# 128-wide attention: projections that begin with half of the turned tiles, a place of their own for the first values' weights, and bias additions inside the first head

## The reference

```python
x = x + _L0_attn_a_ref(_layernorm(x, axis=-1), ...)   # 32 heads of width 16
x = x + _L0_ffn_ref(_layernorm(x, axis=-1), ...)
x = x + _L0_attn_b_ref(_layernorm(x, axis=-1), ...)
x = x + _L0_ffn_ref(_layernorm(x, axis=-1), ...)
x = x + _L1_attn_a_ref(_layernorm(x, axis=-1), ...)   # the step that changes
x = x + _L1_ffn_ref(_layernorm(x, axis=-1), ...)
x = x + _L1_attn_b_ref(_layernorm(x, axis=-1), ...)
x = x + _L1_ffn_ref(_layernorm(x, axis=-1), ...)
```

```python
q = hidden_states @ Wq + bq          # 32 heads of 128
k = hidden_states @ Wk + bk          #  8 heads of 128
v = hidden_states @ Wv + bv          #  8 heads of 128
...                                  # _rope(x): [x1 cos - x2 sin, x1 sin + x2 cos]
scores = einsum('bgrsd,bgtd->bgrst', qg, k) / sqrt(128)
probs = softmax(where(causal, scores, lowest))
ctx = einsum('bgrst,bgtd->bgrsd', probs, v)
return ctx @ Wo + bo
```

## Time and profile before

| what | us |
|---|---|
| median of three runs | 2809.57 (2801.65 to 2809.91) |
| the profiled execution | 2806.13 |
| its span, first to last instruction | 2804.4 |
| the stage of the 128-wide attention, start of its first transfer | 598.0 |
| its last scores | 1654.0 |

### The profile page before, as it was taken

The page is one execution under the profiler, slowest core; times in us unless marked ns, Lnnn a source line. Parts: engine busy times, 40 slices in busy tenths (PEclk is TensorE's granted clock), DMA queues, the critical chain, the costliest instruction groups (busy, mean ns, idle before and its releaser), DMA issues. The chain is left out here.

```text
span 2804.4 us, 41981 instructions
## 1 busy us (share of the span) xinstructions
PE 2549.3 (91%) x14502; PEld 1758.5 (63%) x14502; DVE 1904.1 (68%) x3382; ACT 1495.5 (53%) x2528; POOL 824.3 (29%) x777
## 2 busy tenths in 40 slices
PE   7899988878999999999999987899878999868995
PEld 5444444546888888888888864566554454445663
DVE  6888623445767777777777676677678886366774
ACT  5677821215555555555555541466447778315663
POOL 1200001024535344534345310355412000004552
PEclk9899998989999999999999997999988999889998
DMA  4000000010000000000000012988820000229887
GB/s 156 1 1 1 1 18 20 18 38 23 23 17 27 16 23 24 20 23 23 16 23 23 13 44 86 326 213 196 181 95 1 1 2 1 98 105 313 196 202 205
DMA packets 68190, 197.42 MB, mean 70 GB/s; under 512 B 9040, under 2 KB 9936, under 8 KB 62608
## 3 DMA queue, kind: packets, MB, share of 16 engines
q1 hardware_dynamic: 46928, 145.44, 15.3%
q0 software_dynamic: 21056, 49.30, 9.4%
HBM read 154.33 MB, written 40.37 MB: 69 GB/s over the span
## 5 line engine op out<-in xcount | busy, mean ns | idle before, releaser
L1430 ACT ACTIVATE L1a_ph<-single 128x512 fp32r<-128x512 f32 (+3 forms) x384 | 174.4, 489 | 180.0 <-PE single L1517 179.3
L1571 DVE TENSOR_TENSOR L1a_pl<-single,L1a_ph 128x512 fp32r<-128x512 f32 (+3 forms) x384 | 199.6, 549 | 52.7 <-ACT L1a_ph L1430 52.1
L1587 DVE SCALAR_TENSOR_TENSOR x<-single,L1a_rinv,x 128x512 f32<-128x512 f32 x256 | 189.5, 745 | 58.5 <-PE single L1181 58.2
L1421 ACT ACTIVATE L1a_probs<-pair,L1a_least 128x128 f32<-128x128 f32 (+7 forms) x256 | 190.1, 744 | 71.4 <-DVE L1a_least L1565 69.8
L1565 DVE TENSOR_REDUCE L1a_least<-pair 128x1 f32<-128x128 f32 (+7 forms) x256 | 190.8, 751 | 42.8 <-PE pair L1506 42.2
L1398 POOL TENSOR_TENSOR L1a_swapped<-L1a_swapped,L1a_sin 128x512 f32<-128x512 f32 x80 | 129.2, 1615 | 302.5 <-ACT L1a_swapped L1462 302.5
L793 DVE TENSOR_REDUCE L0a_least<-single 128x1 f32<-128x512 f32 (+3 forms) x304 | 186.4, 658 | 37.6 <-PE single L615 20.7
L793 DVE TENSOR_REDUCE L1b_least<-single 128x1 f32<-128x512 f32 (+3 forms) x304 | 186.2, 657 | 37.8 <-PE single L615 20.8
L496 ACT ACTIVATE L0a_probsT<-pair 128x896 f32<-128x896 f32 (+2 forms) x192 | 149.0, 811 | 59.2 <-PE pair L635 47.1
L496 ACT ACTIVATE L1b_probsT<-pair 128x896 f32<-128x896 f32 (+2 forms) x192 | 149.0, 811 | 59.2 <-PE pair L635 47.0
L1517 PE MATMUL single<-ident,L1a_probs 128*128 128x128 f32 x1152 | 168.9, 274 | 1.4 <-ACT L1a_probs L1421 1.4
(11 more groups left out here) (517 smaller groups left out, 6931.0 us busy)
## 6 DMA issues: line engine op xcount, KB each, us to landing
L1f_wd<-in_L1f_w SPq DMA_DIRECT2D x48, 512.0 KB
L1g_wd<-in_L1f_w SPq DMA_DIRECT2D x48, 512.0 KB
L1a_raw<-in_L1a_w SPq DMA_DIRECT2D x80, 256.0 KB, 2.6
L1f_store<-in_L1f_w SPq DMA_DIRECT2D x16, 1024.0 KB, 8.4
L1g_store<-in_L1f_w SPq DMA_DIRECT2D x16, 1024.0 KB, 9.2
sum<-L0a_pad_row SPq DMA_DIRECT2D x2, 2304.0 KB, 16.4
sum<-x SPq DMA_DIRECT2D x16, 256.0 KB
x<-sum SPq DMA_DIRECT2D x16, 256.0 KB, 5.0
```

The lines of the kernel that those rows point to most:

```text
L1421: act.activation(probs[:, u % 2, 0:n], g.pair[u % 2][:, 0:n], ACT.Exp, bias=least[:, u % 4:u % 4 + 1], scale=-1.0, accum_out=rsum[:, h % 2 ...
L1430: act.activation(p_tile(ph, u, i), turned_bank(u, i), ACT.Copy).then_inc(p_high, 1)
L1571: dve.tensor_tensor(p_tile(pl, u, i), turned_bank(u, i), p_tile(ph, u, i).bitcast(F32), ALU.subtract)\
L1587: dve.scalar_tensor_tensor(out=g.x[:, t, :], in0=aux_bank(("O", h, t)), scalar=rinv[:, h % 2, t:t + 1], in1=g.x[:, t, :], op0=ALU.mult, op ...
```

## The change

Four things are edited, all in the stage `L1a`:

1. TensorE's turning of a tile becomes a step `x` of its table. Six tiles are turned, then comes the first keys' projection (tokens 0 to 511, which are tiles one to four), then the last two tiles. Each projection waits for the split tiles that it reads: four for a first half, eight for a second.
2. The first values' weights get the place of the odd output weights, number 4, so that they need not wait for the keys' weights. The opening now has the first values' projection and its turning, and both halves of the first queries.
3. The first head gets a table of its own, `FIRST_HEAD`; all later heads keep `SCHEDULE`.
4. GpSimd's eight bias additions go from the opening into the first head, and VectorE's output additions of that head wait for their own tile only.

```diff
 OPENING = {
-    "PE": "K0 Q0 K1 s s Q1",
-    "ACT": "K0 Q0 K1 e Q1",
-    "DVE": "K0a K0b Q0a Q0b m K1a K1b m Q1a Q1b",
-    "POOL": "w w x x x x x x x x K0a K0b Q0a Q0b K1a K1b w Q1a Q1b w w",
+    "PE": "x x x x x x K0 x x Q0 K1 V0 v0 Q1",
+    "ACT": "K0 Q0 K1 V0 v0 Q1",
+    "DVE": "K0a K0b Q0a Q0b v0 K1a m K1b Q1a m Q1b",
+    "POOL": "w w w w K0a K0b Q0a K1a Q0b w Q1a K1b Q1b",
+}
+FIRST_HEAD = {
+    "PE": ("s V1 s t s", "v1 Q0 t s", "s t Q1 W1p t s", "s t W0", "s", "O6p t O7p O5p O1 s", "O4p O0", "t s O2 t O3"),
...
+    "POOL": ("Q0a", "x x Q0b w", "x x", "x", "", "x w x", "Q1a", "x"),
 }
...
-    rows = [(-1, OPENING[engine])] + [(h, text) for h in range(HEADS128) for text in SCHEDULE[engine][h % GH]]
+    rows = [(-1, OPENING[engine])]
+    for h in range(HEADS128):
+        rows += [(h, text) for text in (SCHEDULE[engine][h % GH] if h else FIRST_HEAD[engine])]
...
-                of = {"Q": of + 1, "K": of // GH + 1}.get(kind, of // GH)
+                of = {"Q": of + 1, "K": of // GH + 1}.get(kind, max(of, 0) // GH)
...
 def weight_slot(piece):
     kind, n = piece
+    if piece == ("V", 0):
+        return 4
...
-                for t in range(NT):
-                    if t >= 2:
-                        pe.wait_ge(x_split, t - 1)
-                    ln_turn(pe, g, ln, t)
-                pe.wait_ge(x_split, NT)
...
+                    if s[0] == "x":
+                        if s[1] >= 2:
+                            pe.wait_ge(x_split, s[1] - 1)
+                        ln_turn(pe, g, ln, s[1])
+                    elif s[0] == "s":
...
                         pe.wait_ge(w_split, SPLIT_NO[piece_of(s)])
+                        pe.wait_ge(x_split, (s[2] + 1) * BLK)
...
                         if h == 0:
-                            dve.wait_ge(biased, NT)
+                            dve.wait_ge(biased, t + 1)
```

More of the change, by code:

```diff
@@ L1492, in _ @@
                         bank_free(s)
-                    if s[0] == "s":
+                    if s[0] == "x":
[3 more added lines that the diff above has]
+                    elif s[0] == "s":
                         u = s[1]
```

## The result

The change takes the median from 2809.57 us (10 runs, 2801.65 to 2814.72) to 2794.11 us (10 runs, 2790.45 to 2800.44): a ratio of 0.995, with a 95% interval of 0.9940 to 0.9961. That is 15.5 us; the interval allows 11 to 17. The forecast was 2792, between 2785 and 2800.

The account below looks back on a forecast made before the run. TensorE's idle time and low clock in the 128-wide attention's opening were taken as the loss. 4.64 + 1.12 + 38.05 + idle (2.0 + 0.5 + 0.8) = 47.1 us against 62.87, 15.8 less: 2792 us, range 2785 to 2800.

Parts of the forecast that it names:

- The sum: From the sixth turned tile's end to the second head's row: 47.1 us against 62.87 before, 15.8 us less.
- the gap for the queries: TensorE's 5.66 us idle ahead of the first scores, for rotated queries: gone, replaced by about 2.0 us before the values' transposes.
- First projection: TensorE's first keys' projection, started right behind the sixth tile at the low clock: 4.64 us, bounds 2.84 and 5.7.
- Clock behind the gap: TensorE's work after the 2.0 us gap ahead of the values' transposes was counted at full clock, a projection at 2.84 us.
- rival of the low clock: Low clock stays longer in the opening, costing 5 us: gain 10 to 11, 2796 to 2797 us; chance 0.14.
- Small waits: TensorE's remaining waits through the first head: 0.3, 0.3 and 0.2, 0.8 us in all, bounds 0 and 4.
- The rival of the softmax: Each of the first head's eight units waits 1.43 us for its exponential, costing 11.4: gain 4, 2803 us; chance 0.10.
- Keys' bias step: ScalarE's first keys' bias step starts at 622.1 us against 625.16 before, 3 us earlier, after splitting tiles seven and eight.
- The table load: ScalarE's load before the first exponential ends at 638.5 us; between 0 and 0.45 us may follow it, 0 taken.
- Hidden, with about 1.5 us to spare: GpSimd's moved additions in the first head: second head's last low queries done at 670.5 us, wanted near 672.
- the rival of a late GpSimd: GpSimd's 17 instructions slow to 1.8 us beside VectorE, late for the second head by 6 us: gain 10, 2797; chance 0.08.
- The six tiles: TensorE's turning of the first six tiles, up to 615.74 us: the change moves nothing there.

Follow-up runs that it names:

- the run with the additions in gaps: Changed kernel with GpSimd's eight bias additions moved to where GpSimd idles in the opening; stage 1054.9 us, against 1058.1 for the changed kernel.
- The run with half of the tiles alone: Kernel before with only the first projection behind six turned tiles and the other two tiles behind it; stage 1068.8 us, against 1074.5 before.
- the run with the scaling later: Changed kernel with VectorE's scaling of the query bias behind the sixth tile's split instead of ahead of the third row; stage 1059.0 us.
- the two reordered openings: Changed kernel with values projected before the second keys (stage 1057.7 us); or with additions in idle gaps, scaling later, first keys' steps before the last tiles' split (1054.4).

## Why the prediction was right, and where it was not

**The sum.** 47.1 us stood for the stretch from the sixth tile to the second head's row; 46.5, 46.2 and 46.9 were measured. The order came out as read: projection at once, tiles behind it, four pieces of weights split by 615.3, the gap for the queries gone, a gap of 2.15 us (forecast 2.0) ahead of the transposes. The terms were less exact than the sum:

- First projection: taken as 4.64, measured 3.88 (615.56 to 619.44). The row of 0.40 at 617.81 shows the clock up 2.2 us after the start, where the earlier trace rows needed 3.93. In the other runs of this order it took 3.1 to 4.7: the same term, with a spread that a single row couldn't show.
- Clock behind the gap: taken as full, but it fell. The projection behind the transposes took 4.39 us (631.49 to 635.88) instead of 2.84, 1.55 more. This is one part of the rival of the low clock, and I had named its reason: a gap between 1.41 and 3.45. The two rows of the granted clock, before the gap's end and after it:

```profile
629.00:631.00 2.00, 0.00 (x0) 0.00 (x0) 1.12 (x2) 1.89 (x3) 0.98 (x2) 1.00 0.00 0
...
632.00:633.00 1.00, 1.00 (x4) 0.74 (x3) 0.50 (x1) 0.47 (x1) 1.00 (x2) 0.50 0.00 0
```

While TensorE idled the clock was at its upper level, and at the lower one, 1.2 GHz, when the work had started again.

- Small waits: 0.8 taken, next to none measured. TensorE is busy 20.00 of 20 us from 640 to 660. The rival of the softmax (1.43 us in each unit) is refuted by that row: in the first head no exponential but the first is waited for (0.35 us).

Too long by 0.8 and 0.8, too short by 1.55: they cancel.

**Keys' bias step.** Predicted 6.4 us behind the sixth tile's end; it came 5.1 behind it (621.04). ScalarE's rows show why:

```profile
620.07 1.09 ACT L1167 ACTIVATE L1a_xh<-single 128x512 fp32r<-128x512 f32 x2 [3.53 <-PE single L141]
621.04 0.69 ACT L1469 ACTIVATE L1a_lin<-single,L1a_bias 128x512 f32<-128x512 f32 x1
...
628.13 0.69 ACT L1469 ACTIVATE L1a_lin<-single,L1a_bias 128x512 f32<-128x512 f32 x1 [2.77 <-POOL L1a_kl L1414]
...
630.24 0.69 ACT L1459 ACTIVATE L1a_vT<-single,L1a_bias 128x512 f32<-128x512 f32 x1
...
638.18 1.28 ACT L1431 ACT_TABLE_LOAD   x1
639.48 0.37 ACT L1431 ACTIVATE L1a_probs<-pair,L1a_least 128x128 f32<-128x128 f32 x1
```

The two copies run together in 1.09 us as soon as the tiles are turned, and the eighth was turned 4.6 us behind the sixth (620.47), not 5.8. From the keys' first bias step to their second it is 7.09 us, as the 7.05 of the earlier trace rows. The values' bias step ends at 630.93, and TensorE starts at 631.07: the gap has the cause that was named.

**The table load.** The load ends at 639.46 and the first exponential starts at 639.48, with no idle time between them, so nothing follows a load here. All ten runs of the new order have it so, within 0.02 us. The Trainium skill, page "ScalarE: Activation LUTs", section "What ACT_TABLE_LOAD costs", adds 1.38 us of drain to the load; by it, as an estimate, the exponential would have started at 640.8. The measurement decides: not in this place.

**The second head: the step that failed.** "Hidden, with about 1.5 us to spare" was wrong, and this part cost 2.4 us (996.3 against 993.9). First GpSimd, then VectorE:

```profile
646.80 1.31 POOL L1408 TENSOR_TENSOR L1a_swapped<-L1a_swapped,L1a_sin 128x512 f32<-128x512 f32 x1 [3.15 <-ACT L1a_swapped L1472]
648.06 3.45 POOL L1403 TENSOR_TENSOR x<-x,L1a_bo 128x512 f32<-128x512 f32 x2
...
656.08 5.02 POOL L1403 TENSOR_TENSOR x<-x,L1a_bo 128x512 f32<-128x512 f32 x4
...
667.43 1.75 POOL L1395 TENSOR_TENSOR L1a_wh<-L1a_raw,ones 128x512 fp32r<-128x512 f32 x1
...
670.57 1.72 POOL L1414 TENSOR_TENSOR L1a_ql<-L1a_lin,L1a_qh 128x512 fp32r<-128x512 f32 x1
672.25 1.30 POOL L1408 TENSOR_TENSOR L1a_swapped<-L1a_swapped,L1a_sin 128x512 f32<-128x512 f32 x1
```

```profile
666.33 1.69 DVE L1614 TENSOR_TENSOR L1a_lin<-L1a_lin,L1a_swapped 128x512 f32<-128x512 f32 x1 [1.21 <-POOL L1a_swapped L1408]
668.05 1.41 DVE L1618 CAST L1a_qh<-L1a_lin 128x512 fp32r<-128x512 f32 x1
...
673.65 0.69 DVE L1614 TENSOR_TENSOR L1a_lin<-L1a_lin,L1a_swapped 128x512 f32<-128x512 f32 x1 [2.16 <-POOL L1a_swapped L1408]
...
674.80 0.66 DVE L1588 TENSOR_TENSOR L1a_cl<-single,L1a_ch 128x512 fp32r<-128x512 f32 x1
```

Two errors lie in the step. The low queries are done at 672.29, not 670.5. From 646.80 GpSimd works through 18 instructions, 25.1 us of work, with one pause of 0.37; I had counted 17 and no pause, and 1.37 for their mean was nearly right (1.40). TensorE wants them at 671.98 and waits 0.36.

The larger error is that only this one consumer was followed. Behind the low queries stands the product by the sine for the third head's queries (first half of the tokens), at 672.25. VectorE waits 2.16 us for it, and in VectorE's queue the low part of the first head's weighted values (L1588) stands behind that addition, although it has nothing to do with it: ScalarE had written the last of its inputs by 672.27. The output product on TensorE needs this part, ready at 675.46, and starts at 675.57 after 1.47 us of idle time. The profile puts that idle time to "issue", so the releaser is my reading of the two timelines; that the additions are the cause is shown by the three runs without them there, whose rest of the stage is 993.9 to 994.2. Measured from start to start against the run with the additions in gaps, the two stops cost 0.6 and 1.7 us: this is the whole 2.4.

Was it the rival of a late GpSimd? In its place, yes; not in its size (5 to 6 us) nor in its reason (slower instructions). The additions took 1.25 to 1.7 us each.

**The six tiles.** The forecast let nothing change ahead of the sixth tile's end. Measured were 10.5, 10.0 and 9.4 before and 7.9, 8.7 and 8.8 after, about 1.5 us of gain that was in no term. Part of it is luck of one load, the output bias, for which VectorE waits ahead of its third row (it landed after 7.9, 7.4 and 7.2 us before and 6.2, 6.7 and 7.2 after), part is VectorE's third row, which no longer runs beside GpSimd's additions (0.53 instead of 1.50). The run with half of the tiles alone tells them apart: its load took 6.2 us as in the changed kernel's first profile, its additions were still in the opening, and its six tiles took 8.9 against 7.9.

**The balance** of the two profiles: 16.4 us in the counted stretch and 2.6 in the six tiles, less 2.4 behind the second head's row and 0.2 ahead of the first tile, is 16.4, where 15.8 was forecast. The number was right partly because an unseen gain and an unseen loss were of like size.

## What to carry to other kernels

When work is moved into an engine's row further on, follow every product of that row to its consumer, and there what stands behind it in the queue: here the wanted result was late by 0.4 us, and a result further down, through another engine's queue, by 1.5. Put such filler where the profile shows the engine idle for longer than the filler takes, not where it is merely not yet waited for. A resource (a buffer place) can be worth nothing in one order and 7.5 us in another, so try it together with the order that needs it.

## What the runs showed of the hardware

- The clock behind a gap of about 2 us is not settled by the gap's length. Ahead of the same transposes it fell behind 2.10, 2.10, 2.15, 2.15, 2.88 and 5.52 us, and stayed behind 2.13 and 2.17, and behind 1.73 and 0.87 in the two reordered openings. A fall costs 1.6 us here: 4.81 us from the transposes to the first score instead of 3.23. Nor did it fall at one moment: in three of these runs it was still at its upper level when TensorE began again, and fell about 0.35, 0.9 and 1.3 us later (estimates, from a mean granted clock of 0.71 and 0.96 from 631 to 632 in two profiles of the changed kernel, where work began at 631.07 and 631.06, and of 0.62 from 632 to 633 in the run with the scaling later, where it began at 630.91). What decides between 2.13 and 2.15 stays open; no run was made for it.
- GpSimd and VectorE slow one another in some pairs and not in others. VectorE's rotation addition took 1.69 us beside GpSimd's last bias addition and a piece of weights, and 0.69 without, its cast 1.41 and 0.43, its normalised row 1.50 and 0.53; GpSimd's own work took 1.72 to 1.75 there instead of 1.28. Beside VectorE's work on PSUM GpSimd's four additions took 5.02 us, 1.25 each. The slow rows look like turns taken: GpSimd's bias addition ends at 667.47, the rotation addition that had started at 666.33 ends 0.55 us later, the weights' instruction of 667.43 ends 1.16 behind that, and the cast of 668.05 ends 0.28 behind that, each a little less than its own length alone (0.69, 1.29 and 0.43) after the one before. This is my reading of one place; no run was made for it. The Trainium skill, page "GPSIMD Engine Reference", section "1. Specifications", names two kinds of VectorE instructions that contend with GpSimd: those with two inputs in SBUF, and those in a two-port mode. The trace agrees for the rotation addition, which has two such inputs; the cast and the normalised row have one, and whether they ran in that mode no row shows.
